# Six places in turn for ScalarE's normalised images, where four were shared by two convolutions

## What is computed

```python
def _gn(v, G=32, eps=1e-5):
    g = v.reshape(B_, G, C_ // G, H_, W_)
    m = jnp.mean(g, axis=(2, 3, 4), keepdims=True)
    s = jnp.var(g, axis=(2, 3, 4), keepdims=True)
    return ((g - m) / jnp.sqrt(s + eps)).reshape(v.shape)
...
x = x + _L0_conv_ref(_gn(x), L0_conv_k)        # 3x3, one kernel a channel
x = x + _L1_conv_ref(_gn(x), L1_conv_weight)   # 7x7, the mean of its four rotations
```

## Time and profile before

| | us |
|---|---|
| median of 3 runs | 3320.15 (3318.07 to 3320.52) |
| the profiled execution | 3324.27 |
| its span, first to last instruction | 3322.5 |
| VectorE busy | 2768.8 |
| TensorE busy | 2873.4 |
| ScalarE busy | 2176.0 |
| GpSimd busy | 2127.9 |

### The profile page before, as it was taken

The page is one execution under the profiler, slowest core; times in us unless marked ns, Lnnn a source line. Parts: engine busy times, 40 slices in busy tenths (PEclk is TensorE's granted clock), DMA queues, the critical chain, the costliest instruction groups (busy, mean ns, idle before and its releaser), DMA issues.

```text
span 3322.5 us, 76555 instructions
## 1 busy us (share of the span) xinstructions
PE 2873.4 (86%) x28676; PEld 1813.7 (55%) x28676; DVE 2768.8 (83%) x5180; ACT 2176.0 (65%) x3969; POOL 2127.9 (64%) x2321
## 2 busy tenths in 40 slices
PE   0468989998999999999999899999989989999996
PEld 0245555565555555555555555555555555555553
DVE  3567888889888889888988988888898888898885
ACT  1355676676667667667666766666766766676672
POOL 3245666766766666666676676676667667666763
PEclk9889999999999999999999999999999999999998
DMA  2699888888888888888888888888888888888866
GB/s 88 163 229 233 219 221 225 223 219 217 224 218 230 228 218 216 223 218 216 230 223 218 220 222 215 227 226 226 220 217 218 224 224 220 224 222 222 219 168 167
DMA packets 966522, 712.46 MB, mean 214 GB/s; under 512 B 102918, under 2 KB 904710, under 8 KB 966086
## 3 DMA queue, kind: packets, MB, share of 16 engines
q1 hardware_dynamic: 511494, 383.52, 45.4%
q10 hardware_dynamic: 405504, 201.38, 21.4%
q0 software_dynamic: 49152, 122.65, 16.0%
HBM read 259.73 MB, written 220.81 MB: 145 GB/s over the span
## 4 chain that ended last, share of the span: by engine, by line
DVE 49%; DMA 13%; issue 13%; POOL 10%; ACT 5%; PE 5%; SPq 4%; ACTq 1%; DVEq 0%; POOLq 0%
DMA BT<-H 12%; DVE X L492 9%; DVE H L465 9%; DVE BN L474 8%; DVE BT L498 8%; POOL H L625 7%; DVE X L443 4%; PE PS L747 3%; SPq L248 2%; PE PS L718 2%; POOL BT L638 2%; POOL H L646 2%; ACT Z L524 2%; ACT H L541 1%; DVE TMP L423 1%
## 5 line engine op out<-in xcount | busy, mean ns | idle before, releaser
L718 PE MATMUL PS<-H,BAND 128*128 128x512 f16 x6912 | 1609.2, 393 | 90.3 <-DMA BAND<-rows 72.2
L718 PEld LDWEIGHTS PS<-H,BAND 128*128 128x128 f16 x6912 | 1026.2, 151 | 628.5 <-issue 125.1
L747 PE MATMUL PS<-BT,BAND 118*32 118x512 f16 x21504 | 1245.8, 389 | 95.6 <-DMA BT<-H 40.8
L646 POOL TENSOR_TENSOR H<-Z,H 128x512 f16<-128x512 f32 x768 | 835.7, 1099 | 677.5 <-ACT Z L544 676.5
L747 PEld LDWEIGHTS PS<-BT,BAND 118*32 118x32 f16 x21504 | 767.3, 131 | 560.1 <-issue 200.3
L625 POOL TENSOR_SCALAR H<-X,RB 128x512 f16<-128x512 f32 x768 | 798.7, 1048 | 341.3 <-DVE RB L432 318.6
L541 ACT ACTIVATE H<-X,RB 128x512 f16<-128x512 f32 x768 | 618.8, 806 | 497.9 <-DVE H L465 425.3
L498 DVE COPY BT<-BT 39x8512 f16<-39x8512 f16 x192 | 465.0, 2422 | 296.1 <-DMA BT<-H 292.2
L524 ACT ACTIVATE Z<-X,RB 128x512 f32<-128x512 f32 x768 | 563.0, 804 | 105.7 <-DVE RB L432 83.5
L544 ACT ACTIVATE Z<-X,RB 128x512 f32<-128x512 f32 x768 | 615.5, 801 | 0.0
L567 ACT ACTIVATE DUMP<-X 128x512 bf16<-128x512 f32 x768 | 475.8, 620 | 132.7 <-DVE X L492 132.2
(11 more groups left out here) (48 smaller groups left out, 503.0 us busy)
## 6 DMA issues: line engine op xcount, KB each, us to landing
X<-in_x SPq DMA_DIRECT2D x768, 256.0 KB, 5.0
out_y<-X ACTq DMA_DIRECT2D x768, 256.0 KB, 5.5
BT<-H POOLq DMA_DIRECT2D x384, 162.1 KB, 5.2
BT<-H POOLq DMA_DIRECT2D x384, 149.6 KB, 5.8
BT<-H SPq DMA_DIRECT2D x576, 99.8 KB
BT<-H SPq DMA_DIRECT2D x384, 62.3 KB
BT<-H SPq DMA_DIRECT2D x192, 83.1 KB
rows<-v_all SPq DMA_DIRECT2D x8, 1638.0 KB, 11.8
```

The lines of the kernel that those rows point to most:

```text
L646: g.tensor_tensor(part(H1, n, 1, img, O1, P1), Z[:, img, :].rearrange("p (c w) -> p c w", c=CC), part(H1, n, 0, img, O1, P1), ALU.subtract ...
L718: last = mm(PA[:, ch, :], band[:, j, ws, :], data[:, :, O1 - 1 + j:O1 - 1 + j + W], start=k == 0, stop=k == 3 * K1 - 1)
L747: last = mm(banks2(n)[b * BL:(b + 1) * BL, ch, :], band[:, j, :], rows, start=j == 0, stop=j == K2 - 1, tile_position=(0, b * BL))
```

## The change

Z gets six places. Each normalised image has a running number: turn by turn the four images of line 524, then the four of line 544; its place is the number modulo 6. ScalarE waits, just ahead of the activation that writes Z, until the image six numbers earlier has been read. The high part of line 541 has no wait on Z any more.

```diff
+ZR = 6
...
-        Z = sb("Z", [P, NI, CC * W], F32)
+        Z = sb("Z", [P, ZR, CC * W], F32)
...
+        def z1(n, img):
+
+            return 2 * NI * (n - 1) + NI + img
+
+        def z2(n, img):
+
+            return 2 * NI * (n + 3) + img
...
+            def wait_z(k):
+
+                k -= ZR
+                while k >= z1(0, 0):
+                    turn, place = divmod(k, 2 * NI)
+                    if place < NI and real(turn - 3):
+                        act.wait_ge(lo_done[1], NI * (turn - 3) + place + 1)
+                        return
+                    if place >= NI and real(turn + 1):
+                        act.wait_ge(lo_done[0], NI * (turn + 1) + place - NI + 1)
+                        return
+                    k -= ZR
...
-                    if real(n + 3):
-                        act.wait_ge(lo_done[0], m + 3 * NI + img + 1)
-                    else:
-                        act.wait_ge(lo_done[1], m - NI + img + 1)
-                    nc.scalar.activation(Z[:, img, :].rearrange("p (c w) -> p c w", c=CC), xs(n, img),
+                    wait_z(z2(n, img))
+                    nc.scalar.activation(zbuf(z2(n, img)), xs(n, img),
...
-                if real(n - 4):
-                    act.wait_ge(lo_done[1], m - 4 * NI + img + 1)
-                elif n > 0:
-                    act.wait_ge(lo_done[0], m - NI + img + 1)
                 nc.scalar.activation(part(H1, n, 0, img, O1, P1), xs(n, img), ACT.Identity,
                                      bias=rb[:, 1, img:img + 1],
                                      scale=rb[:, 0, img:img + 1]).then_inc(hi_done[0], 1)
-                nc.scalar.activation(Z[:, img, :].rearrange("p (c w) -> p c w", c=CC), xs(n, img),
+                wait_z(z1(n, img))
+                nc.scalar.activation(zbuf(z1(n, img)), xs(n, img),
```

More of the change, by code:

```diff
@@ L178, in part, with zbuf @@
             return H[:, n % 2, which, :, off + img * pitch:off + img * pitch + W]
+        def z1(n, img):
+            return 2 * NI * (n - 1) + NI + img
+        def z2(n, img):
+            return 2 * NI * (n + 3) + img
+        def zbuf(k):
+            return Z[:, k % ZR, :].rearrange("p (c w) -> p c w", c=CC)
         def banks2(n):
@@ L464, in slot @@
                         dve.wait_ge(hi_done[1], m + 1)
-                        v.tensor_tensor(part(H2, n, 1, img, O2, P2),
-                                        Z[:, img, :].rearrange("p (c w) -> p c w", c=CC),
+                        v.tensor_tensor(part(H2, n, 1, img, O2, P2), zbuf(z2(n, img)),
                                         part(H2, n, 0, img, O2, P2), ALU.subtract).then_inc(lo_done[1], 1)
@@ L513, in _ @@
         def _(act):
+            def wait_z(k):
[9 more added lines that the diff above has]
+                    k -= ZR
             def normalise2(n, at):
-                m = NI * at(n)
                 rb = RB[:, 1, (n // CPU_) % 2]
                 for img in range(NI):
-                    if real(n + 3):
-                        act.wait_ge(lo_done[0], m + 3 * NI + img + 1)
-                    else:
-                        act.wait_ge(lo_done[1], m - NI + img + 1)
-                    nc.scalar.activation(Z[:, img, :].rearrange("p (c w) -> p c w", c=CC), xs(n, img),
+                    wait_z(z2(n, img))
+                    nc.scalar.activation(zbuf(z2(n, img)), xs(n, img),
                                          ACT.Identity, bias=rb[:, 1, img:img + 1],
@@ L645, in low_parts1 @@
                     wait_apart(pool, hi_done[0], NI * at(n) + img + 1)
-                    g.tensor_tensor(part(H1, n, 1, img, O1, P1), Z[:, img, :].rearrange("p (c w) -> p c w", c=CC),
+                    g.tensor_tensor(part(H1, n, 1, img, O1, P1), zbuf(z1(n, img)),
                                     part(H1, n, 0, img, O1, P1), ALU.subtract).then_inc(lo_done[0], 1)
```

## The result

| us | before | after |
|---|---|---|
| median | 3320.34 (3318.07 to 3321.26) | 3431.82 (3427.98 to 3450.31) |
| ratio after / before | | 1.0348 [1.0316, 1.0380] |
| the profiled execution | 3324.27 | 3450.31 |
| its span | 3322.5 | 3448.5 |

The change makes the kernel 3.5% slower, 3432 us where 3302 was predicted. (Medians of four executions each. The profiled one of the kernel after is the longest of its four, 18 us above the median, so the 126 us between the two spans are more than the 111 between the medians.) It went to the side of rival R1, and 77 us beyond R1's own price. The lines have moved: 443, 465, 482, 484, 492, 498 on VectorE are now 456, 478, 494, 496, 504, 510; 422 and 423 are 435 and 436; GpSimd's 625, 638, 646 are 641, 654, 662; ScalarE's 524, 541, 544, 555 are 544, 556, 560, 571.

The account below looks back on a forecast made before the run. The prediction took the time as VectorE's own turns B and C, plus A's chain from VectorE through GpSimd's high parts and gather to the copy. Its terms, -40 + 22 + 0 = -18 us, gave 3302 us; range 3270 to 3344.

Parts of the forecast that it names:

- R1: Rival, chance 0.25: GpSimd cuts into VectorE's line 465 in turn C, 0.83 us in 64 cycles, +53 us; 3355 us.
- Part 4: Turn C: GpSimd asks amid VectorE's four images of line 465; cost taken as 0, upper end 0.83 us per cycle.
- turn 69: Traced turn before the change: GpSimd's high part waited 2.31 us until VectorE's three images ended, VectorE losing nothing.
- C: Third turn of the cycle of three; 14.58 us, VectorE busy 13.86, in the cycle shown before the change.
- B: Second turn of the cycle of three; 16.95 us, VectorE busy 16.13, in the cycle shown before the change.
- A: First turn of the cycle (number a multiple of 3); 16.27 us, VectorE busy 12.96, waiting for the high parts' gather.
- Part 3: Turn B: lines 482 and 484 wait on GpSimd, 0.36 us in 61 cycles, +22 us; line 465's 0.4 us absorbed.
- Part 1: Turn B: ScalarE and GpSimd start earlier once the wait goes; GpSimd reaches its high parts 1.6 us earlier each cycle.
- Part 2: Turns B into C: lines 422 and 423 no longer wait for GpSimd's high parts, saving 40 us of VectorE's time.
- R2: Rival, chance 0.15: queued stores take back ScalarE's lead, lines 422 and 423 wait again; no change, 3320 us.
- R3: Rival, chance 0.15: A's gather lands earlier, half a microsecond a cycle off the copy's wait, -32 us; 3270 us.
- The mark that the prediction named: Turn A: VectorE's image 0 just held some 0.02 us by GpSimd: let in, 50 cycles; not held: GpSimd waited, 13.

Follow-up runs that it names:

- e14: Changed kernel with GpSimd's low parts waiting for VectorE's four low parts, but in turn B only for line 456; 3406.64 us, ratio 1.0237.
- e13: Changed kernel with GpSimd's low parts waiting for two of VectorE's four low parts; 3361.26 us, ratio 1.0119.
- e6: Kernel before, still four places, with only ScalarE's wait on Z moved behind the high part; 3367.59 us, ratio 1.0135.
- e1: Changed kernel, six places, with the old wait back ahead of every ScalarE high part; 3341.58 us, ratio 1.0016.
- e3: Changed kernel, six places, with the old wait back in turns A and B, so the change acts in C alone; 3436.59 us, ratio 1.0309.
- e2: Changed kernel plus one GpSimd wait, before its first low part of a turn, for VectorE's four low parts; 3316.78 us, ratio 0.9954.
- e4: Changed kernel, six places, with the old wait back in turn C alone, so the change acts in A and B; 3350.02 us, ratio 1.0071.
- e12: Kernel before plus two GpSimd waits, so it stands still during VectorE's small steps (482/484 and 422/423); 3312.55 us, ratio 0.9969.

## Why the prediction was wrong

**The step that failed is the choice of 0 in Part 4.** The trace of before had two outcomes for a GpSimd instruction that arrives during VectorE's row, and the choice went to turn 69 by a likeness: a row that nobody had just held. In both outcomes, though, the arrival was the same, a high part 0.05 to 0.07 us behind the start of the row. In C a low part was to arrive 0.8 us into the row, and with images still to start behind it the trace of before had no low part at all. The likeness doesn't carry over: what was put at 0 measured 1.79 us a cycle, 115 us. Low parts that arrived in a row whose first image was undisturbed (0.68 us), with GpSimd idle before them (2.44, 3.03, 3.64 and 3.88 us after line 456 or 443 began, in e14, after, e13 and e6), were served at the next image boundary: in all 59 C turns of after, e13 and e6, and in the 34 turns of e14 that began so. In the late B turns, where a low part follows its own gather issue directly, it didn't even wait for the boundary (1.11 us in turn 88), and VectorE lost more. The rule cited from the Trainium skill there, page "SBUF — State Buffer", section "Who interferes with whom", read strictly (whoever has the port pair has it for one whole instruction), was right for these low parts, and R1, built on it, was the right mechanism; the trace of turn C agrees with 1.48 us for 1.09, the 0.4 being the rest of VectorE's image. The high parts of turn A, held for three images, still don't follow it so read.

**R1's price was less than half.** It counted one entry in a cycle at 0.83 us. One entry costs 0.90: close. But VectorE, made longer by the first, is still in its row when GpSimd's second low part comes 1.44 us behind: two entries, 1.79 us, and 115 us in 64 cycles. With that C grew from 14.61 to 16.36 us, and B, which was to shrink, grew from 16.97 to 17.54: both of the prediction's own signs of being wrong. The prediction had every number for it: VectorE's row of 2.49 us, GpSimd's two arrivals 1.42 apart, and the 0.83 that the first adds. It stopped at the first.

**In B, Part 3 saw one meeting, and a harmless one.** It has GpSimd's first low part from 1581.65, ahead of line 465, costing 0.4 that a later wait absorbs. That is what happened in 14 of 59 turns, with 0.30. In 30 the gather ended too late, by some 1.7 us, and the low parts came in the midst of the row: 3 us. It is late where the high part at the end of A meets the copy (2.97 for 0.76 in turn 88, the same kind of collision as the earlier trace rows). Such turns are few where B is as before (5 of 59 in before, 6 in e1, 7 in e3) and many where ScalarE is free in B (29 in after, 24 in e2, 19 in e4). The high part is held 0.4 us longer in A, but that alone doesn't do it: e1 holds it just so, and is late in 6 turns. The copy must come early too, and it does where A's gather lands early: 6.2 us after its last issue in the late turns of after and of e4, 8.0 and 8.3 in the others. Why it lands early in some turns was not found out. In e2 the late gather harms nobody, for the low parts wait anyway. Part 1 took its gain "in each cycle" and held the gather in its place.

**What held.** Part 1: GpSimd's low parts end 1.14 us earlier in B and 1.50 in C (means; 1.6 was forecast). Part 2: lines 422 and 423 gave back 39.2 us (40 forecast). Part 3's 22 us for 482 and 484, after the change 494 and 496: in the kernel after it was -22.4, as VectorE came later there and met less; in e2, where VectorE's row is undisturbed, the two hold 72.6 us against 63.5, so +9, with 496 at 813 ns as forecast (0.75 us). The term had the right sign there and was more than twice too large: 482, which was to stay at 0.6 to 0.9 us, fell to 0.32. Turn B "shrinks by some 0.3 us": 16.97 to 16.65 in e2. The forecast of 3302 is an 18 us gain; e2, which has the change without the cut-ins, gains 15 (0.46% of 3320). That the two are so near is in part luck: in e2 the two terms of the sum measure -35 and +9, so -26 us, and the profiled executions differ by 10. What the sum left out gives the rest back, in the main these three: A's row is 21 us shorter, VectorE waits 28 us more for A's high part, and its copies take 11 us more (465.0 to 475.5).

**R2** was partly there: in turn 88 the third store's issue took 2.60 us and ScalarE's fourth image waited 1.17 for it. It didn't take back the lead. **R3** was there in part: A's gather landed 7.1 us after its last issue on average, for 7.8, the copy's wait fell by 19.5 us, and turn A shrank by 0.24 us a cycle, 15 us in all, where R3 had 32. Its early landings are also what brings copy and high part together, and makes B's gather late, so R1's loss in B falls in the turns in which R3 came true. The range, 3270 to 3344, left R1 out beyond "four cycles of five" of one entry; even R1 as priced, 3355, lay outside.

**How far the 126 us are explained.** VectorE is 129.9 us busier; at line 478 it waits 28.0 us more for the high part in A, before the copy 19.5 less: 138.4. That is 12 us more than the 126; VectorE's other gaps are shorter by as much, the largest part at line 433, before's 420 (17.4 to 11.4 us). DMA sets in which turns B's gather is late, but what these cost VectorE is seen at line 478: e2 has 24 such turns and no loss.

## What to carry to other kernels

Before freeing an engine from a wait, ask what it will then land beside, and follow each later arrival of it with the row already lengthened by the first, not the first arrival alone. An order between two engines that exclude each other may be worth keeping even where no data asks for it: here one wait on GpSimd, for VectorE's last image, made a change of +3.5% into one of -0.5%, the best ratio of the kernels measured that compute the whole (e12's interval overlaps with its own). When a trace shows two outcomes of one collision and nothing in it says why, the range must hold both at their full price.

## What the runs showed of the hardware

- VectorE's row of two-input images (128x512 float32 to float16, 0.68 us each) lets in a GpSimd low part at the next image boundary, where it arrived 0.17 to 1.6 us behind the start of the row and GpSimd was idle before it. Each entry costs VectorE 0.90 us for a GpSimd instruction of 1.09, and 0.42 for one of 0.62: some 0.2 us less than the instruction takes by itself.
- Where GpSimd's low part followed its gather issue directly at 3.23 us, VectorE's running image was the one that took 2.04, a loss of 1.36. The low part took 1.11 us, so it didn't wait, and the image ended 0.56 us behind it; in C the lengthened image ends 0.55 behind the low part that came in. So the image seems to have run only when the low part was through; why isn't shown.
- Once, in turn 28 of after, three low parts whose data was ready ran one behind the other (1.10 us each) while one image of VectorE lasted 4.28 us: VectorE didn't get in between them. Images of 4.1 to 4.3 us are also in e3, e4 and e14, one or two each.
- In A a high part that arrives 0.06 us behind the start of VectorE's row is held for three images, in 60 of 60 turns of after, e1 and e2; in before a high part at the same distance was held in 12 of 60 and let in after two images in 48. The mark that the prediction named goes with this in 838 of the 840 A turns of all fourteen kernels: held where VectorE's first image took 0.68 to 0.69 us (484 turns), let in where it took 0.69 to 0.71, in ns 678 to 690 against 694 to 709; in the other two the high part came ahead of the row. It doesn't go with it for low parts: in e14 one 0.17 us behind the start is let in after one image of 0.68. **What separates the two is open.** That GpSimd's instruction is right behind another of its own isn't enough: in turn 88 its second low part was, and it got in. The form of the instruction, what GpSimd did before it, and the 0.1 us weren't tried apart.
- A one-element VectorE instruction with two scalars from memory takes 267 ns, more than one of four elements with two tensors (162 to 164 ns undisturbed); GpSimd doesn't stretch it.
- VectorE time won at the small steps comes back poorly (10 of 82 us in e12) while the copies, C's above all, wait for gathers that the same edit makes later.
